# Turning denominators and router weights on VectorE in 32x32 blocks instead of on TensorE, in a two-layer transformer kernel

## The reference, cut to what matters

```python
# layer 0
attn = jax.nn.softmax(sim, axis=-1)
out = jnp.einsum('bwij,bwje->bwie', attn, bv)        # divided by a denominator per token and head
weights = jnp.zeros_like(router_probs).at[jnp.arange(T)[:, None], topk_idx].add(topk_probs)
expert_out = jnp.einsum('teh,ehd->ted', h1, rw2) + rb2[None]
mixed = jnp.einsum('ted,te->td', expert_out, weights)
# layer 1
topk_w = topk_w / (topk_w.sum(-1, keepdims=True) + 1e-20)
topk_w = topk_w * ROUTED_SCALING
final = (gathered * topk_w[:, :, None]).sum(1)
```

## Time and profile before

| | |
|---|---|
| median of 3 runs | 977.98 us (976.25 to 978.58) |
| the profiled execution | 976.32 us |
| its span, first to last instruction | 975.0 us |
| busy: PE, DVE, ACT, POOL | 952.0, 666.1, 505.4, 434.6 us |
| mean granted clock of PE | 0.999 |

### The profile page before, as it was taken

How to read it: one execution, slowest core, us unless ns; L and a number is a source line. 1 busy time by engine, 2 the same in 40 slices (tenths; PEclk the granted TensorE clock), 3 DMA queues, 4 the chain that set the end, 5 groups by cost and what they waited for, 6 DMA issues and landing times.

```text
span 975.0 us, 13550 instructions
## 1 busy us (share of the span) xinstructions
PE 952.0 (98%) x4508; PEld 633.6 (65%) x4508; DVE 666.1 (68%) x1578; ACT 505.4 (52%) x1165; POOL 434.6 (45%) x343
## 2 busy tenths in 40 slices
PE   5899999999999999999999999999999999999998
PEld 3565566676666766677666766667666676656765
DVE  6957769687665876767866677757777477724943
ACT  3574783536746266462764537545465454745222
POOL 5858247551094401863036620566206651054443
PEclk9999999999999999999999999999999999999999
DMA  7050240613423034230442306332053220543061
GB/s 284 12 174 1 35 130 0 144 44 10 133 68 98 22 13 133 72 93 21 38 129 76 88 1 91 76 95 68 1 99 90 65 66 2 107 102 87 23 164 33
DMA packets 63381, 72.80 MB, mean 75 GB/s; under 512 B 33288, under 2 KB 34312, under 8 KB 62928
## 3 DMA queue, kind: packets, MB, share of 16 engines
q1 hardware_dynamic: 61744, 69.81, 31.0%
q10 hardware_dynamic: 1568, 2.13, 0.6%
HBM read 69.04 MB, written 2.88 MB: 74 GB/s over the span
## 4 chain that ended last, share of the span: by engine, by line
PE 88%; DVE 7%; ACT 2%; issue 2%; DMA 0%; POOL 0%; DVEq 0%; ACTq 0%
PE ps L648 12%; PE ps L765 12%; PE ps L503 10%; PE ps L505 9%; PE ps L504 9%; PE ps L557 6%; PE ps L570 6%; PE ps L584 5%; PE ps L656 3%; PE ps L740 2%; PE ps L773 1%; PE ps L498 1%; PE ps L538 1%; PE ps L729 1%; PE ps L528 1%
## 5 line engine op out<-in xcount | busy, mean ns | idle before, releaser
L1167 ACT ACTIVATE wide<-ps 128x512 f32<-128x512 f32 x136 | 80.9, 595 | 208.8 <-PE ps L505 208.2
L1093 ACT ACTIVATE pw<-ps,w_cols 128x512 f32<-128x512 f32 x144 | 98.5, 687 | 98.6 <-PE ps L505 97.2
L1054 ACT ACTIVATE pw<-ps,nmax 128x256 f32<-128x256 f32 x256 | 117.5, 473 | 51.1 <-DVE nmax L1420 46.6
L648 PE MATMUL ps<-pw,w_w 128*128 128x512 f32 x288 | 135.4, 592 | 0.0
L1907 POOL TENSOR_TENSOR atc<-atc,wide 128x512 f32<-128x512 f32 x64 | 82.0, 1282 | 119.8 <-DVE atc L1634 119.8
L1887 POOL TENSOR_TENSOR kr<-qks,w_rope 128x512 f32<-128x512 f32 x32 | 43.8, 1367 | 158.3 <-DVE qks L1398 158.2
L1436 DVE COPY pt<-ps 128x512 f32<-128x512 f32 x126 | 81.7, 679 | 26.5 <-PE ps L570 26.3
L503 PE MATMUL ps<-yc,eg 128*128 128x512 f32 x128 | 94.4, 738 | 0.0
L1907 POOL TENSOR_TENSOR pt<-pt,wide 128x512 f32<-128x512 f32 x48 | 61.7, 1284 | 66.4 <-DVE pt L1634 65.3
L1420 DVE TENSOR_REDUCE nmax<-ps 128x4 f32<-128x1024 f32 (+1 forms) x80 | 79.1, 1006 | 13.8 <-PE ps L557 13.7
L648 PEld LDWEIGHTS ps<-pw,w_w 128*128 128x128 f32 x288 | 53.5, 189 | 42.6 <-issue 37.7
(11 more groups left out here) (229 smaller groups left out, 2131.0 us busy)
## 6 DMA issues: line engine op xcount, KB each, us to landing
wb<-scratch SPq DMA_DIRECT2D x128, 256.0 KB, 4.0
wb<-scratch SPq DMA_DIRECT2D x32, 512.0 KB, 5.9
wide<-scratch SPq DMA_DIRECT2D x16, 512.0 KB, 5.7
xin<-in_x SPq DMA_DIRECT2D x8, 256.0 KB, 2.7
out<-wide SPq DMA_DIRECT2D x7, 256.0 KB, 10.3
wb<-in_w SPq DMA_DIRECT2D x1, 1152.0 KB, 8.5
w_w<-in_w SPq DMA_DIRECT2D x1, 1152.0 KB, 12.4
w_ed<-in_ed SPq DMA_DIRECT2D x1, 1024.0 KB, 15.7
```

The costliest lines, as they stand in the source:

```text
L648: pe.matmul(bank(k), w2[:, e, c, :], hid[:, n % 4, :], start=c == 0, stop=c == 1 and e < E0).then_inc(*DOWN0.one)
L1054: m = act.activation(pw[:, u % 2, j, :], ps[:, score_bank(u, par), qt * SEQ:(qt + 1) * SEQ], ACT.Exp, bias=nmax[:, u % 3, j:j + 1], scale= ...
L1093: act.activation(hid[:, n % 4, :], bank(UPS0[n % 2]), ACT.Gelu, bias=cols[:, C_B1 + 2 * e + c:C_B1 + 2 * e + c + 1], scale=1.0).then_inc(* ...
```

## The change

PE's three turnings and ACT's three copies go. In their place DVE turns each table with one instruction (`dve.transpose`, a STREAM_TRANSPOSE), which transposes every block of 32x32 by itself: from `rden` to `denc` and from `wr0` to `wc0`, 128 partitions x 32, and from `wr1` to `wc1`, 128 x 128. `rden` is laid out as head, tile for this. The partition 32g+r of the result then holds row r of the turned table for the tokens 32g to 32g+31 of every tile, so a new helper `rows_out` stores it in 4 transfers, one for each g, in runs of 128 bytes: 32 runs per transfer for the two tables of layer 0, 128 runs for that of layer 1. The straight store of 4-byte runs (L390) goes too: all 8 steps take the new way. DVE waits for its own writes ahead of each transpose (`own`, or a wait on `INVERTED`), and the next round's table waits until the last store of it has landed (`SCRATCH0`, `SCRATCH1`, `SCRATCH2` now count four transfers). `weigh0` loses its wait for `SCRATCH2`, ACT's `affine1(0)` its wait for `DEN_COPIED`.

```diff
+        denc = sb("denc", [P, HEADS * TILES])
...
+            def rows_out(scratch, columns, rows, done):
+
+                for g in range(BLOCKS):
+                    part = columns[BLOCK * g:BLOCK * g + BLOCK]
+                    dst = bass.AP(tensor=scratch.tensor, offset=BLOCK * g, ap=rows + [[1, BLOCK]])
+                    sp.dma_start(dst, part).then_inc(*done.one)
+
...
             def weights_layer0_out(s):
-
+                w.wait_ge(*WEIGHTS0.at(s))
                 if s:
-                    w.wait_ge(*WEIGHTS0.at(s))
-                else:
-                    w.wait_ge(*WT0.at(s))
-                for k in range(RING):
-                    w.wait_ge(*(wb_layer0(k, 0) if s == 1 else wb_layer1(RING + k, s - 2)) if s else (WB[k], 0))
-                if s:
-                    by_token = bass.AP(tensor=scratch0.tensor, offset=0, ap=[[1, P], [P, E0 * TILES]])
-                    with nc.allow_non_contiguous_dma(reason="a weight of 4 bytes goes to each row"):
-                        sp.dma_start(by_token, wr0[:, :, :].rearrange("p e t -> p (e t)")).then_inc(*SCRATCH0.one)
-                else:
-                    sp.dma_start(scratch0, wt0[:, :]).then_inc(*SCRATCH0.one)
+                    for k in range(RING):
+                        w.wait_ge(*(wb_layer0(k, 0) if s == 1 else wb_layer1(RING + k, s - 2)))
+                rows_out(scratch0, wc0, [[P, E0 * TILES]], SCRATCH0)
...
-                    w.wait_ge(*WT1.at(s))
+                    w.wait_ge(*WEIGHTS1.at(s))
...
-                    sp.dma_start(scratch1, wt1[:, :]).then_inc(*SCRATCH1.one)
+                    rows_out(scratch1, wc1, [[TOK, E1], [P, TILES]], SCRATCH1)
...
-                w.wait_ge(*DEN_COPIED.at(s))
+                w.wait_ge(*DEN_TURNED.at(s))
                 w.wait_ge(*DEN_WIDE.at(s - 1))
-                sp.dma_start(scratch2, wden).then_inc(*SCRATCH2.one)
+                rows_out(scratch2, denc, [[P, HEADS * TILES]], SCRATCH2)
...
-            def turn_denominators(s, k):
-                w.wait_ge(*INVERTED.at(s))
-                take(k)
-                for t in range(TILES):
-                    m = pe.transpose(bank(k)[0:HEADS, t * P:(t + 1) * P], rden[:, t, :], ident[:, :])
-                m.then_inc(*DEN_TURNED.one)
-                freed[k] = DEN_COPIED.at(s)
...
-            def denominators(s, k):
-                w.wait_ge(*DEN_TURNED.at(s))
-                copy(wden, bank(k)[0:HEADS, :], DEN_COPIED)
...
-                    w.wait_ge(*DEN_COPIED.at(1))
...
-                dve.reciprocal(rden[:, 2 * g:2 * g + 2, 2 * p:2 * p + 2].rearrange("p q h -> p h q"),
+                dve.reciprocal(rden[:, 2 * p:2 * p + 2, 2 * g:2 * g + 2],
                                den[:, u % 3, :].rearrange("p (h q) -> p h q", q=2)).then_inc(*INVERTED.one)
+                if u == UNITS - 1:
+                    w.wait_ge(*INVERTED.at(s))
+                    w.wait_ge(*SCRATCH2.at(s - 1))
+                    dve.transpose(denc[:, :], rden[:, :, :].rearrange("p h t -> p (h t)")).then_inc(*DEN_TURNED.one)
...
-                dve.scalar_tensor_tensor(
+                own(dve.scalar_tensor_tensor(
                     out=wr0[:, :, :].rearrange("p e t -> p t e"), in0=mr0[:, :, :], scalar=TAKEN, in1=pr0[:, :, :],
-                    op0=ALU.is_equal, op1=ALU.mult).then_inc(*WEIGHTS0.one)
+                    op0=ALU.is_equal, op1=ALU.mult))
+                dve.transpose(wc0[:, :], wr0[:, :, :].rearrange("p e t -> p (e t)")).then_inc(*WEIGHTS0.one)
 
...
+                w.wait_ge(*SCRATCH1.at(s - 1))
...
-                    in1=spread(sm1[:, :], [(1, TILES), (0, E1)]), op0=ALU.mult,
-                    op1=ALU.mult).then_inc(*WEIGHTS1.one)
+                    in1=spread(sm1[:, :], [(1, TILES), (0, E1)]), op0=ALU.mult, op1=ALU.mult))
+                dve.transpose(wc1[:, :, :].rearrange("p t e -> p (t e)"),
+                              wr1[:, :, :].rearrange("p t e -> p (t e)")).then_inc(*WEIGHTS1.one)
```

More of the change, by code:

```diff
@@ L30 @@
 RING = 4
+BLOCKS, BLOCK = 4, 32
 EPS = 1e-5
@@ L165, in two_layers @@
         wr0 = sb("wr0", [P, E0, TILES])
-        wt0 = sb("wt0", [E0, TOK])
+        wc0 = sb("wc0", [P, E0 * TILES])
         qka = sb("qka", [P, 2, TOK])
@@ L178, in two_layers @@
         den = sb("den", [P, 3, 4])
-        rden = sb("rden", [P, TILES, HEADS])
+        rden = sb("rden", [P, HEADS, TILES])
+        denc = sb("denc", [P, HEADS * TILES])
         atc = sb("atc", [P, 4, TOK])
@@ L207, in two_layers @@
         wr1 = sb("wr1", [P, TILES, E1])
-        wt1 = sb("wt1", [E1, TOK])
+        wc1 = sb("wc1", [P, TILES, E1])
         def half_pt2(r):
@@ L269, in two_layers @@
         OUT = event("out", 1, 16)
-        SCRATCH0, SCRATCH1, SCRATCH2 = (event(n, 1, 16) for n in ("scratch0", "scratch1", "scratch2"))
+        SCRATCH0, SCRATCH1, SCRATCH2 = (event(n, BLOCKS, 16) for n in ("scratch0", "scratch1", "scratch2"))
         DEN_WIDE = event("den_wide", 2, 16)
@@ L292, in two_layers @@
         EXPS, TRANSPOSED, PT = (event(n, 2 * UNITS) for n in ("exps", "transposed", "pt"))
-        DEN_TURNED, DEN_COPIED, NORMALISED = event("den_turned"), event("den_copied"), event("normalised", PAIRS)
-        LOGITS0, LOGITS0_ROWS, LOGITS0_LESS, EXP0, WEIGHTS0, WEIGHTS0_TURNED, WT0 = (event(n) for n in (
-            "logits0", "logits0_rows", "logits0_less", "exp0", "weights0", "weights0_turned", "wt0"))
+        DEN_TURNED, NORMALISED = event("den_turned"), event("normalised", PAIRS)
+        LOGITS0, LOGITS0_ROWS, LOGITS0_LESS, EXP0, WEIGHTS0 = (event(n) for n in (
+            "logits0", "logits0_rows", "logits0_less", "exp0", "weights0"))
         UP0, GELU, DOWN0 = (event(n, 2 * (E0 + 1)) for n in ("up0", "gelu", "down0"))
@@ L299, in two_layers @@
         LAY0, ROWS0, X1, X1S = event("lay0"), event("rows0"), event("x1"), event("x1s")
-        LOGITS1, TANH1, WEIGHTS1, WEIGHTS1_TURNED, WT1 = (
-            event(n) for n in ("logits1", "tanh1", "weights1", "weights1_turned", "wt1"))
+        LOGITS1, TANH1, WEIGHTS1 = (event(n) for n in ("logits1", "tanh1", "weights1"))
         UV, UV_SILU, AFFINE, SWAPPED1, TURNED1, ROPED1 = (event(n, k) for n, k in (
@@ L616, in logits0 @@
                 freed[k] = LOGITS0_ROWS.at(s)
[L618 to L624, removed]
             def up0(s, e):
@@ L693, in logits1 @@
                 freed[k] = TANH1.at(s)
-            def turn_weights1(s, k):
-                w.wait_ge(*WEIGHTS1.at(s))
-                take(k)
-                for t in range(TILES):
-                    m = pe.transpose(bank(k)[0:E1, t * P:(t + 1) * P], wr1[:, t, :], ident[:, :])
-                m.then_inc(*WEIGHTS1_TURNED.one)
-                freed[k] = WT1.at(s)
             def uv(s, c, i, k):
@@ L798, in attention @@
                         scores(s, u + 2)
-                    if u == 5 and first:
-                        turn_weights0(s, score_bank(5, 1))
                     if u == 4 and second:
@@ L959, in experts1 @@
                 up1(x, 15)
-                if not more:
-                    turn_weights1(s, 6)
                 down1(x, 13)
@@ L1076, in exp0 @@
                 act.activation(pr0[:, :, :], lg0[:, :, :], ACT.Exp).then_inc(*EXP0.one)
-            def wt0_copy(s, k):
-                w.wait_ge(*WEIGHTS0_TURNED.at(s))
-                copy(wt0[:, :], bank(k)[0:E0, :], WT0)
             def gelu(s, e):
@@ L1128, in tanh1 @@
                 act.activation(er1[:, :], bank(k)[:, 0:TILES * E1], ACT.Tanh, scale=0.5).then_inc(*TANH1.one)
-            def wt1_copy(s, k):
-                w.wait_ge(*WEIGHTS1_TURNED.at(s))
-                w.wait_ge(*SCRATCH1.at(s - 1))
-                copy(wt1[:, :], bank(k)[0:E1, :], WT1)
             def uv_silu(s, c, i, dst, k):
@@ L1186, in attention @@
                         exp0(s)
-                    if u == 6 and first:
-                        wt0_copy(s, score_bank(5, 1))
                     if u == 5 and second:
@@ L1203, in attention @@
                     out_cols(s, 3)
-                    denominators(s, 6)
                     gelu_half(s, 0, 0)
@@ L1298, in experts1 @@
                 silu(x, 15)
-                if not more:
-                    wt1_copy(s, 6)
                 if more:
@@ L1498, in weigh0 @@
                     w.wait_ge(*WEIGHED.at(s))
-                else:
-                    w.wait_ge(*SCRATCH2.at(s))
-                    if e == 2 and s:
-                        w.wait_ge(*Y0_TURNED.at(s))
-                    if e > 2:
-                        w.wait_ge(*ADDED0.at(s, e - 3))
+                if e == 2 and s:
+                    w.wait_ge(*Y0_TURNED.at(s))
+                if e > 2:
+                    w.wait_ge(*ADDED0.at(s, e - 3))
                 dve.scalar_tensor_tensor(
```

8 lines of the change are left out of this document (removed).

## The result

The changed kernel takes 970.85 us in the median (970.42 to 971.25, 4 runs), the kernel before 977.24 (976.25 to 978.58, 4 runs): ratio 0.9937, 95% interval 0.9921 to 0.9953. The span of the profiled execution goes from 975.0 to 969.1 us, by 5.9.

The account below looks back on a forecast made before the run. PE's instruction stream was taken as the bound from step 2 on. Removed groups gain 4.97 us, DVE transposes cost 1.16, net 3.8: median 977.98 to 974.2 us, range 972.3 to 977.7.

Parts of the forecast that it names:

- PE is the bound, what is taken out there is won: From step 2 on PE's instruction stream is the time, busy 117.95 of a 118.12 us step; removed groups gain 4.97 us.
- A group is worth 0.35 or 0.36 us by starts, not by durations: Four PE transposes, start to next start: seven denominator groups give 2.45 us, seven layer 1 weight groups 2.52 us.
- DVE's transposes at 0.22 and 0.30, 0.27 or 0.35 a place: Added transposes plus 0.05 us wait show once in step 0, twice in step 1, once ending step 7: 1.16 us.
- rival of a collision with POOL: In step 0 POOL's weight splitting holds a DVE transpose, about 1.0 us more, 975.2 us; chance 0.13.
- What is hidden: Steps 2 to 7: transposes ahead of `z0_low` hide in its 4.19 us wait; layer 0's 0.27 in 0.39 us slack.
- the 2.1 us of slack: Last step: the hidden row is ready at 937.1 and PE takes it at 939.23, so a late `wb` is covered.
- The 4-byte store "becomes short, but nothing on the chain waited for the loads behind it": Layer 0 weights' store, for which SP waited 75.1 us in seven steps; shortening it was given no gain.
- Late short stores, the rival of the other side: 128-byte-run stores land as slowly as the 4-byte one, last step's `wb` 13.9 us late, 986 us; chance 0.06.

Follow-up runs that it names:

- the slots put back: Changed kernel with all 17 groups of 4 transposes put back on PE, turning the identity into unread banks: 977.08 us, 5.5 over the changed kernel.
- this table alone: Kernel before, only the layer 0 weights of steps 1 to 7 turned on DVE and stored in 128-byte runs, PE's groups kept: 976.47 us, ratio 0.9938.
- the run with four transfers: Changed kernel, but layer 0 weights in steps 1 to 7 stored in 4-byte runs, as four transfers of 1024 runs: 1026.74 us.
- the kernel with the stop of 2.02 us: Changed kernel with every transpose on DVE made four times in a row, each waiting for the one before: 976.09 us, 4.5 over the changed kernel.

## Why the prediction was wrong

The direction was no luck: the forecast's own terms, as measured, make 5.8 - 0.7 = 5.1 of the 5.9 us. What made the number wrong is a path that I priced at nothing and two terms of the sum.

- *PE is the bound, what is taken out there is won.* Right: the slots put back cost 5.5 us.
- *A group is worth 0.35 or 0.36 us by starts, not by durations.* Right for denominators. For the layer 1 weights the term was too small: 0.44, since the first product behind a group also starts its successor 0.08 late, and in step 1 more. I measured from the group to the next start and should have measured over the next two. That is 0.6 us over seven slots, and 0.2 more in step 1, of the 2.1 missed in the pair of traces (5.9 for 3.8); the median moved by 0.5 more, since the trace of before is one of its faster runs.
- *DVE's transposes at 0.22 and 0.30, 0.27 or 0.35 a place.* Right in size (0.21, 0.21, 0.31 us; +0.26, +0.23, +0.30 at three places, and 0.24, 0.25, 0.38 for each one more). In step 0 the term failed: 0.27 was charged, -0.11 came, 0.4 us of the miss. I read the chain of the earlier trace rows as DVE's own from 46.88 on, while one pass in it (L1349) waits for POOL: it took 0.79 us before and 0.46 after, 0.64 to 0.79 in the four traces without the transpose ahead of it and 0.46 to 0.62 in the ten with it. My rival of a collision with POOL had the transpose held, and none was (0.21 us). The first 20 us are another 0.14.
- *What is hidden.* Right, and with more cover than I read: the layer 0 table in steps 2 to 7 stood three more transposes without a trace on PE, so 0.39 us was not the end of its slack. DVE's wait in front of chunk 0 of the last step grew from 1.57 to 2.11 us, by 0.5 of the 2.1 us of slack.
- *The 4-byte store "becomes short, but nothing on the chain waited for the loads behind it".* This step failed. The sentence is true and priced the store at nothing, since I looked for its cost only among those who wait for it. The cost lay with those who don't: ACT, DVE and through them PE stood still for parts of its flight. In the pair of traces of the result that is 0.73 us; from this table alone, 5.3 us where the experiments ran. There the rest of the change is worth 4.9 us (976.47 less 971.55); if it was worth as much in the runs of the result, 1.5 of the 6.4 us remain for the store. That is an estimate.
- *Late short stores, the rival of the other side.* It did not come: the short stores kept SP 1.2 us. The 3 to 4 ns a run that I took from the earlier trace rows (2.6 in the mean) are not the price of a run but of neighbouring ones, and too low, since SP began to wait only some 7 us behind the issue. Apart, 4096 runs kept SP 3.6 us.
- Two signs were there before: runs that lay 2.3 us apart with PE at 98%, and the copy of `atc` that started late. No term of the sum could have made either.

**What stays open.** By which path a store holds ACT and DVE. In three of the six long holds of the run with four transfers (steps 4, 5 and 6) no packet of the instruction queues is under way, so a late load of code is not needed for one; in the other three there is one, and it takes 3.1 to 9.9 us where the median of that trace is 0.9. Both engines waited for PE's signals, and PE ran on for a while, which fits signals that arrive late, but no run separates that from another cause. Open too are why before takes 4.6 us more in the experiments than in the runs of the result (the chip of those is not known, and the three of the experiments agree within 0.4), why 16 bytes of gap are enough, why four transfers of 1024 runs cost 55 us and one of 4096 8.8, and why removing the store gives 5.3 us from the kernel before but adding it costs 8.8 in the changed one.

## What to carry to other kernels

A transfer that nobody waits for can still set the time: look at what all engines do while it is in flight, and take an engine that starts late behind a finished releaser, or a scatter of some us, as a sign. Four-byte stores side by side from many partitions were such a transfer here; turn the table on chip, or if it must be scattered, leave 16 bytes or more from run to run, the least that did no harm here. Price a removed group on PE by starts, over the two instructions behind it. Before you charge a cost to a chain on DVE, look for a pass in it that lasts longer than its size asks and ends with one of POOL's.

## What was not expected of the hardware

- One and the same number of 4-byte runs kept SP 13.7 us a time side by side and 3.6 at 64 bytes; split into four transfers it kept SP 18.1 us and held ACT and DVE for up to 9.5 us.
- Stops of PE of 1.98 and 2.02 us stood in front of a clock at half in three places of two traces, one of 1.27 us did not; and in two of five runs of the kernel with the stop of 2.02 us the mean clock was full.
- A DVE pass of 4 elements took 0.46 to 0.79 us beside a POOL instruction and ended with it in 14 traces, 0.17 us without it in three.
- The kernel with the dense store took 977.2 us in the runs of the result and 981.6 to 982.0 on three chips later, the one without it 970.85 and 971.55.
